# A gated attention layer on one core: x copied into the output early, and the last stage adding to it with accumulating DMAs

## The chip, the core and the metric

The kernel runs on one core of a Trainium2 chip. The core has TensorE (PE in the profile: matmuls; PEld: the loading of their weights), VectorE (DVE), ScalarE (ACT), GpSimd (POOL) and SyncE (SP), and 16 DMA engines that all of them share. SyncE and GpSimd issue the DMAs of this kernel; SyncE's go through the queue that the profile calls q1 (hardware_dynamic), GpSimd's through q0 (software_dynamic). The metric is the device time of one execution in microseconds.

## The reference

For x of 16 sequences of 1024 tokens with 256 features, the output is x plus an attention branch times a gate:

```
xn = layernorm(x)
s  = attention(xn)                        # 16 heads of 16, rope, causal softmax, then @ W_o
h  = leaky(xn @ w_fc[e]) ** 2             # e: the one of 8 experts that the router picks for the token
g  = silu(h @ w_proj[e])
out = x + s * g
```

## The kernel before

The work is cut into 32 tiles (NT) of 512 tokens. A tile in SBUF is 128 partitions by 4 rows of 256 numbers (SUB = 4), 512 KB. Three functions run one after the other.

`project_phase` normalises x, makes q, k, v and the router's choice, and puts each token's row number in the order by experts into `slot` (later called `token_row`).

`attention_phase` goes through 64 groups n, one for each sequence and 4 heads. TensorE makes the scores twice (L1052 for the row maxima, L1118 for the exponentials) and the context (L1094); VectorE takes maxima, ScalarE exponentials. Beside this SyncE works off its own list for each group: `load_max` (L809, 12 KB, which the second scores need), the operands of the group three ahead, `store_ctx` (L813), another `load_max`, another `store_ctx`, and in some groups after that `load_xn` (L816, 512 KB), whose rows GpSimd scatters to their experts (L888).

`expert_output_phase` has two stages. In the first, 72 blocks of 256 tokens go through their experts' weights, and the gates go to `g_dram`, in the order by experts. Meanwhile SyncE loads the context of the first 14 tiles (CR = 14) and x of the first 6 (XR = 6). In the last stage, for each tile t:

- GpSimd issues four indirect DMAs (L1258) that gather the gates of the tile's tokens, 128 rows of 1 KB each, into `gate`, a ring of 4 tiles (GR). Ahead of tile t it waits for `y_used` of tile t-2 (LEAD = 2), the first half of its product.
- TensorE turns the context (L1376) and multiplies it by W_o (L1388) into two halves of 512 columns; ScalarE copies the turned context (L1299).
- VectorE multiplies each half by the gate (L1329, `prod`), waits for x, and adds x in place in `r_sb` (L1334), a ring of 6 tiles.
- SyncE loads the context of tile t+14, stores the tile (L1233) and loads x of tile t+4 (L1210), each as soon as what it needs is there, in this order:

```
            sp.wait_ge(out_ready, 2 * (t + 1))
            sp.dma_start(out[t].rearrange("(s p) d -> p s d", p=P),
                         r_sb[:, t % XR].rearrange("p (s d) -> p s d", s=SUB)).then_inc(out_stored[t % XR], 16)
```

Each engine works off its list in the order in which it is written; semaphores order the engines among each other.

Of the kernel before, what the change touches and what calls it, by code (L numbers as in the profile page):

```python
# [24 lines left out]
ALU = mybir.AluOpType  # L25
ACT = mybir.ActivationFunctionType

P = 128
# [8 lines left out]
SUB = TOK // P  # L37
# [571 lines left out]


def attention_phase(nc, ctx, parts_dram, v_dram, ctx_dram, xn_dram, xs_dram, token_row, w_fc, w_proj, expert_in, first_in,
                    consts):

# [11 lines left out]
    def sem(name):  # L627
        return ctx.enter_context(nc.semaphore(name))
# [47 lines left out]
    scattered = [sem(f"scattered{u}") for u in range(2)]  # L676
    zeros_set = sem("zeros_set")
    xs_cleared = sem("xs_cleared")


    STEPS = []
# [118 lines left out]
    @block.sync  # L800
    def _(sp):
        def load(b, r):
            for i in range(LOADS):
                load_operand(sp, i, parts_dram, v_dram, b, r, q_st[r], k_st[r], v_st[r], operands_loaded[r])

        def load_max(n, r, c):

            sp.wait_ge(max_moved, 2 * n + c + 1)
            sp.dma_start(q_st[r][KS:KM, c, :], max_T[:, c, :]).then_inc(max_loaded[c], 16)  # L809

        def store_ctx(n, b, r, c):
            sp.wait_ge(normalised, 2 * n + c + 1)
            sp.dma_start(ctx_dram[b * TPB + c, :, :, r * GW:(r + 1) * GW], ctx_out[:, c]).then_inc(ctx_stored[c], 16)  # L813

        def load_xn(t):
            sp.dma_start(xn_sb[:, t % 2].rearrange("p s d -> p (s d)"), xn_dram[t]).then_inc(xn_loaded[t % 2], 16)  # L816

        def clear_xs(i):
            sp.dma_start(xs_dram[i * 4 * P:(i + 1) * 4 * P].rearrange("(p a) d -> p (a d)", p=P),
                         zeros[:]).then_inc(xs_cleared, 16)  # L820

        for r in range(1, RING - 1):
            load(0, r)
        load_max(0, 0, 0)
        sp.wait_ge(zeros_set, 1)
        for t in range(2):
            load_xn(t)

        def group(n, b, r, first, last):
            load_max(n, r, 1)  # L830
            r3, b3 = (r + 3) % RING, b + (r + 3) // RING
            if not (isinstance(b3, int) and b3 >= B):
                if not first:
                    sp.wait_ge(pv_done, NS * n)
                load(b3, r3)
            if not first:
                store_ctx(n - 1, b - (1 if r == 0 else 0), (r - 1) % RING, 1)
            if n < CLEAR_GROUPS:
                for i in range(CLEARED // 2):
                    clear_xs(CLEARED * n + i)  # L840
            if not last:
                load_max(n + 1, (r + 1) % RING, 0)
            store_ctx(n, b, r, 0)
            if n < CLEAR_GROUPS:
                for i in range(CLEARED // 2, CLEARED):
                    clear_xs(CLEARED * n + i)
            for s in subs_scattered(n):
                t = s // SUB + 2
                if s % SUB == SUB - 1 and t < NT:
                    sp.wait_ge(scattered[t % 2], 16 * SUB * (t // 2))  # L850
                    load_xn(t)
            if n == EXPERT_WEIGHTS_AT:
                for d in range(DC):
                    sp.dma_start(w_all[:, :, d * HID:(d + 1) * HID],
                                 w_fc[d * P:(d + 1) * P].rearrange("p (e h) -> p e h", e=E)).then_inc(weights_loaded, 16)
                sp.dma_start(w_all[:, :, DC * HID:], w_proj).then_inc(weights_loaded, 16)
            if last:
                for u in range(2):
                    sp.wait_ge(scattered[u], 16 * NT * SUB // 2)
                for m in range(XS):  # L860
                    sp.dma_start(xs_sb[:, m].rearrange("p s d -> p (s d)"), block_rows(xs_dram, m))\
                        .then_inc(xs_loaded[m], 16)

        for n in range(N - RING):
            group(n, n // RING, n % RING, n == 0, False)
        for r in range(RING):
            group((B - 1) * RING + r, B - 1, r, False, r == RING - 1)
        store_ctx(N - 1, B - 1, RING - 1, 1)
        for c in range(HALVES):
            sp.wait_ge(ctx_stored[c], 16 * N)  # L870

# [268 lines left out]
def expert_output_phase(nc, ctx, xs_dram, expert_in, ident, block_expert, g_dram, x, w_o, ctx_dram, token_row,  # L1140
# [10 lines left out]

    RING = 4
    CR, XR = 14, 6
    AHEAD = XR - 2
    LEAD = 2
    BS = BLK // P
    W = SUB * D
# [10 lines left out]
    GR = 4  # L1168
    gate = sb("gate", [P, GR, SUB, D])
    cT = sb("cT", [P, 2, DC, TOK])  # L1170
    prod = sb("prod", [P, 2, W])
    banks = [bank(f"ps_t{i}") for i in range(8)]
    ps_x, ps_h, ps_g = banks[0:2], banks[2:4], banks[4:6]
    ps_cT = [banks[6:8], banks[0:2]]
# [11 lines left out]
    g_stored = [sem(f"g_stored{r}") for r in range(RING)]  # L1186
    wo_loaded = sem("wo_loaded")
    c_loaded = [sem(f"c_loaded{r}") for r in range(CR)]
    x_loaded = [sem(f"x_loaded_o{r}") for r in range(XR)]
    cT_ready = sem("cT_ready")  # L1190
    cT_copied = sem("cT_copied")
    gate_loaded = [sem(f"gate_loaded{r}") for r in range(GR)]
    y_ready = sem("y_ready")
    y_used = sem("y_used")
    out_ready = sem("out_ready")
    out_stored = [sem(f"out_stored{r}") for r in range(XR)]

    block = ctx.enter_context(nc.Block())
# [1 line left out]
    @block.sync  # L1200
    def _(sp):
        def load_xs(n):
            sp.dma_start(xs_sb[:, n % XS].rearrange("p s d -> p (s d)"), block_rows(xs_dram, n))\
                .then_inc(xs_loaded[n % XS], 16)

        def load_ctx(t):
            sp.dma_start(c_sb[:, t % CR], ctx_dram[t]).then_inc(c_loaded[t % CR], 16)

        def load_x(t):
            sp.dma_start(r_sb[:, t % XR].rearrange("p (s d) -> p s d", s=SUB),  # L1210
                         x[t].rearrange("(s p) d -> p s d", p=P)).then_inc(x_loaded[t % XR], 16)

        for n in range(NBLK):
            if n + XS < NBLK:
                sp.wait_ge(xs_turned, n + 1)
                load_xs(n + XS)
            sp.wait_ge(gated, n + 1)
            sp.dma_start(block_rows(g_dram, n), g_sb[:, n % RING].rearrange("p s d -> p (s d)"))\
                .then_inc(g_stored[n % RING], 16)
            if n % 4 == 3 and n // 4 < CR:  # L1220
                load_ctx(n // 4)
            if n == 8:
                sp.dma_start(w_o_sb[:], w_o.rearrange("(c p) n -> p c n", p=P)).then_inc(wo_loaded, 16)
            if n >= NBLK // 2 and n % 4 == 1 and (n - NBLK // 2) // 4 < XR:
                load_x((n - NBLK // 2) // 4)

        for t in range(NT):
            n = t + CR
            if n < NT:
                sp.wait_ge(cT_ready, DC * (t + 1))  # L1230
                load_ctx(n)
            sp.wait_ge(out_ready, 2 * (t + 1))
            sp.dma_start(out[t].rearrange("(s p) d -> p s d", p=P),  # L1233
                         r_sb[:, t % XR].rearrange("p (s d) -> p s d", s=SUB)).then_inc(out_stored[t % XR], 16)
            n = t + AHEAD
            if XR <= n < NT:
                sp.wait_ge(out_stored[n % XR], 16 * (n // XR))
                load_x(n)
        for r in range(XR):
            sp.wait_ge(out_stored[r], 16 * len(range(r, NT, XR)))  # L1240

    @block.gpsimd
    def _(pool):
# [6 lines left out]
                .then_inc(weights_picked, 1)  # L1250
        for r in range(RING):
            pool.wait_ge(g_stored[r], 16 * NBLK // RING)
        for t in range(NT):
            r = t % GR
            if t >= LEAD:
                pool.wait_ge(y_used, 2 * (t - LEAD) + 1)
            for s in range(SUB):
                pool.indirect_dma_start(  # L1258
                    out=gate[:, r, s, :], out_offset=None, in_=g_dram[:, :],
                    in_offset=bass.IndirectOffsetOnAxis(ap=token_row[:, t * SUB + s:t * SUB + s + 1], axis=0))\  # L1260
                    .then_inc(gate_loaded[r], 16)

    @block.scalar
    def _(act):
# [37 lines left out]
    def _(dve):  # L1302
# [19 lines left out]
        for t in range(NT):  # L1322
# [3 lines left out]
            for i in range(2):  # L1326
                cols = slice(512 * i, 512 * (i + 1))
                dve.wait_ge(y_ready, 2 * t + i + 1)
                nc.vector.tensor_tensor(prod[:, u, cols], ps_y[u][i][:], g[:, cols], ALU.mult).then_inc(y_used, 1)  # L1329
            dve.wait_ge(x_loaded[r], 16 * (t // XR + 1))  # L1330
            for i in range(2):
                cols = slice(512 * i, 512 * (i + 1))
                dve.wait_ge(y_used, 2 * t + i + 1)
                nc.vector.tensor_tensor(r_sb[:, r, cols], prod[:, u, cols], r_sb[:, r, cols],  # L1334
                                        ALU.add).then_inc(out_ready, 1)

    @block.tensor
    def _(pe):
# [74 lines left out]
def gated_attention(nc, x, w_all, w_o, w_fc, w_proj, rope, expert_ids, out):  # L1413
# [9 lines left out]
    with ExitStack() as whole:  # L1423
# [6 lines left out]
        expert_in = expert_operands(nc, whole)  # L1430
        with ExitStack() as ctx:
            attention_phase(nc, ctx, parts_dram, v_dram, ctx_dram, xn_dram, xs_dram, token_row, w_fc, w_proj, expert_in,
                            first_in, consts)
        with ExitStack() as ctx:  # L1434
            expert_output_phase(nc, ctx, xs_dram, expert_in, consts[0], block_expert, g_dram, x_t, w_o, ctx_dram,
                                token_row, out_t)
# [41 lines left out]
```

## Time and profile before

| what | value |
|---|---|
| median of 3 runs | 2410.21 us (2407.6 to 2410.84) |
| the profiled execution's own time | 2409.12 us |
| its span, first to last instruction | 2407.4 us |
| mean granted TensorE clock | 0.98 |
| PE, DVE, ACT, POOL busy | 2276.9, 2010.7, 1787.7, 1050.7 us |
| moved by DMA | 406.28 MB |

The span is the profiler's, and 1.7 us of the execution's time lie outside it. Busy times are over all stages: what bounds one stage has to be read from that stage.

### The profile page before, as it was taken

What the parts mean: (1) busy time and instruction counts of PE and PEld (TensorE: products, weight loads), DVE (VectorE), ACT (ScalarE), POOL (GpSimd) and SP (SyncE); (2) the same over time, 40 slices, a digit from 0 to 9 for tenths busy, and PEclk for the clock granted to TensorE, in tenths of its full rate; (3) what the DMA queues carried; (4) which work ended last, traced back from release to release, by engine and by line L of the source; (5) the groups of instructions that cost most, each with busy time, mean ns of one, the idle gap of its engine ahead of it and who ended that gap; (6) DMA issues with size and microseconds to landing.
All of it is one profiled execution on the core that took longest, in us unless ns stands there. A gap on an engine that the chain in (4) does not pass through costs nothing. (4 is left out here: it accounts for less than half of the span.)

```text
span 2407.4 us, 96050 instructions
## 1 busy us (share of the span) xinstructions
PE 2276.9 (95%) x38509; PEld 1342.8 (56%) x38509; DVE 2010.7 (84%) x5739; ACT 1787.7 (74%) x4319; POOL 1050.7 (44%) x1252
## 2 busy tenths in 40 slices
PE   7999994999999999999999999999999999899787
PEld 6777771544545445445454454444454544788676
DVE  7999998999999999999998999999999995454444
ACT  6777771888888888888888888888888888555111
POOL 6999995222223333333333333333332333223666
PEclk9999995999999999999999999999999999999998
DMA  6899885454533433434344334334333331796998
GB/s 215 287 300 301 299 271 164 155 181 164 168 106 99 133 101 103 129 96 128 107 126 130 107 107 127 96 110 124 105 112 111 105 100 30 261 322 246 326 333 262
DMA packets 302572, 406.28 MB, mean 169 GB/s; under 512 B 99248, under 2 KB 233648, under 8 KB 302000
## 3 DMA queue, kind: packets, MB, share of 16 engines
q1 hardware_dynamic: 289840, 366.58, 48.4%
q0 software_dynamic: 12288, 33.57, 4.1%
q8 instruction: 304, 4.98, 0.8%
q14 instruction: 140, 1.15, 0.1%
HBM read 225.46 MB, written 173.02 MB: 166 GB/s over the span
## 5 line engine op out<-in xcount | busy, mean ns | idle before, releaser
L976 DVE CUSTOM_DVE_ANT_0 dump<-ps_rows,mask 128x128 bf16<-128x128 f32 (+7 forms) x2048 | 1471.1, 753 | 132.8 <-issue 108.3
L946 ACT ACTIVATE probs<-ps_cols 128x512 f32<-128x512 f32 (+3 forms) x3072 | 1314.8, 499 | 242.8 <-PE ps_cols L1118 226.5
L1118 PE MATMUL ps_cols<-q_st,k_st 99*32 99x512 bf16 (+3 forms) x12288 | 864.2, 327 | 5.1 <-DMA q_st<-max_T 2.8
L1052 PE MATMUL ps_rows<-k_st,q_st 96*32 96x128 bf16 (+3 forms) x12288 | 817.9, 330 | 18.8 <-DVE row_max L976 7.6
L912 POOL TENSOR_SCALAR_AFFINE_SELECT probs<-probs 128x512 f32<-128x512 f32 x512 | 325.0, 635 | 1039.3 <-ACT probs L946 1034.8
L1094 PE MATMUL ps_ctx<-probs,v_st 128*32 128x512 f32 (+3 forms) x6144 | 633.2, 487 | 1.2 <-POOL probs L912 1.0
L1118 PEld LDWEIGHTS ps_cols<-q_st,k_st 99*32 99x32 bf16 x12288 | 322.1, 95 | 343.7 <-ACT probs L946 173.7
L1052 PEld LDWEIGHTS ps_rows<-k_st,q_st 96*32 96x32 bf16 x12288 | 287.8, 96 | 383.3 <-DVE row_max L976 237.8
L1094 PEld LDWEIGHTS ps_ctx<-probs,v_st 128*32 128x32 f32 x6144 | 168.5, 110 | 92.0 <-POOL probs L912 15.6
L976 DVE DVE_READ_ACCUMULATOR2_ANT row_max<- 128x1 f32 x2048 | 171.8, 84 | 0.0
L1388 PE MATMUL ps_t<-w_o_sb,cT 128*128 128x256 f32 x512 | 128.0, 408 | 31.2 <-DVE prod L1329 29.2
L1258 POOL DMA_INDIRECT gate<-g_dram,slot x128 | 128.5, 1004 | 63.4 <-issue 35.1
L321 POOL TENSOR_TENSOR rest<-roped,parts 128x1024 f32<-128x1024 f32 x64 | 138.2, 2160 | 25.7 <-ACT parts L372 21.1
L888 POOL DMA_INDIRECT xs_dram<-xn_sb,slot x128 | 125.8, 983 | 33.7 <-issue 33.4
L327 POOL TENSOR_TENSOR parts<-rest,parts 128x1024 bf16<-128x1024 f32 x64 | 139.7, 2183 | 0.0
L1299 ACT ACTIVATE cT<-ps_t 128x512 f32<-128x512 f32 x64 | 34.6, 596 | 137.3 <-PE ps_t L1376 137.3
L1329 DVE TENSOR_TENSOR prod<-ps_t,gate 128x512 f32<-128x512 f32 x64 | 41.3, 686 | 112.7 <-DMA gate<-g_dram,slot 112.6
L1388 PEld LDWEIGHTS ps_t<-w_o_sb,cT 128*128 128x128 f32 x512 | 102.6, 206 | 49.7 <-issue 27.6
L378 ACT ACTIVATE parts<-rest 128x1024 bf16<-128x1024 f32 x64 | 67.7, 1058 | 75.7 <-POOL rest L321 75.6
L560 PE MATMUL ps_qk<-xT_hi,w_all_hi 128*128 128x512 f32 x256 | 106.5, 416 | 0.0
L560 PE MATMUL ps_vr<-w_all_hi,xT_hi 128*128 128x264 f32 x256 | 78.3, 306 | 24.0 <-DVE xT_lo L434 23.4
L560 PE MATMUL ps_qk<-xT_hi,w_all_lo 128*128 128x512 f32 x256 | 100.9, 394 | 0.0
(115 smaller groups left out, 2556.5 us busy)
## 6 DMA issues: line engine op xcount, KB each, us to landing
parts_dram<-parts SPq DMA_DIRECT2D x64, 768.0 KB, 4.1
q_st<-parts_dram SPq DMA_DIRECT2D x384, 128.0 KB
k_st<-parts_dram SPq DMA_DIRECT2D x384, 128.0 KB
xs_dram<-zeros SPq DMA_DIRECT2D x36, 512.0 KB, 4.2
xs_sb<-xs_dram SPq DMA_DIRECT2D x72, 256.0 KB, 4.4
g_dram<-g_sb SPq DMA_DIRECT2D x72, 256.0 KB, 3.3
v_dram<-v_sb SPq DMA_DIRECT2D x32, 544.0 KB, 4.9
v_st<-v_dram SPq DMA_DIRECT2D x64, 272.0 KB
```

Of the source, the lines that this page charges most:

```text
L321: nc.gpsimd.tensor_tensor(rest[:, m % 2], roped[:, m % 2].rearrange("p k t -> p (k t)"), parts[:, t % 2, a, 0], ALU.subtract).then_inc(res ...
L327: nc.gpsimd.tensor_tensor(parts[:, t % 2, a, 2], rest[:, m % 2], parts[:, t % 2, a, 1], ALU.subtract).then_inc(part3_done, 1)
L560: mm = nc.tensor.matmul(out, lhs(i, c), rhs(j, c), start=((c, i, j) == PASSES[0]), stop=((c, i, j) == PASSES[-1]))
L888: pool.indirect_dma_start(out=xs_dram[:, :], out_offset=bass.IndirectOffsetOnAxis(ap=token_row[:, s:s + 1], axis=0), in_=xn_sb[:, u, s % S ...
L912: nc.gpsimd.affine_select(out=tri, in_=tri, compare_op=ALU.is_ge, fill=0.0, base=0, pattern=[[0, GH], [1, P]], channel_multiplier=-1).then ...
L946: nc.scalar.activation(probs[:, k % PB, h, 0:w], ps_cols[(GH * k + h) % CB][:, 0:w], ACT.Exp).then_inc(exp_done, 1)
L976: nc.vector.tensor_tensor_reduce(out=dump[:, done % 2, 0:n], in0=ps_rows[:, 512 * bank:512 * bank + n], in1=mask[:, S - n:S], scale=1.0, s ...
L1052: mm = nc.tensor.matmul(ps_rows[a:a + VW, 512 * (bank + c):512 * (bank + c) + w], q_st[r][0:KS, i // IB, q0 + a:q0 + a + VW], k_st[r][0:KS ...
L1094: mm = nc.tensor.matmul(ps_ctx[VW * h:VW * (h + 1), o:o + w], v_st[r][:, j * V_ROW + VP * h:j * V_ROW + VP * h + VW], probs[:, k % PB, h, ...
L1118: mm = nc.tensor.matmul(ps_cols[(GH * k + h) % CB][a:a + VW, 0:w], k_st[r][:, j // IB, k0 + a:k0 + a + VW], q_st[r][:, c, h * 512 + q0 - 5 ...
L1258: pool.indirect_dma_start(out=gate[:, r, s, :], out_offset=None, in_=g_dram[:, :], in_offset=bass.IndirectOffsetOnAxis(ap=token_row[:, t * ...
L1388: mm = nc.tensor.matmul(ps_y[u][i][:, (s % 2) * D:(s % 2 + 1) * D], cT[:, u, c, s * P:(s + 1) * P], w_o_sb[:, c, :], start=(c == 0), stop= ...
```

## The change

x is copied to the output from DRAM to DRAM during attention: SyncE issues a copy of 512 KB at the end of every second group. The last stage then no longer loads x and no longer adds it: VectorE writes the product straight into `r_sb`, and GpSimd issues a DMA for each tile that adds `r_sb` to the output in DRAM (`accum_op`). The ring `prod` and the waits for x go; VectorE waits for a ring place of `r_sb` to have been stored.

```
@@ attention_phase, SyncE
+            if n % TPB == 0:
+                flat = [a[n // TPB].rearrange("(p s) d -> p (s d)", p=P) for a in (out, x)]
+                sp.dma_start(*flat).then_inc(out_filled, 16)
...
+        sp.wait_ge(out_filled, 16 * NT)
@@ expert_output_phase, SyncE
-            if n >= NBLK // 2 and n % 4 == 1 and (n - NBLK // 2) // 4 < XR:
-                load_x((n - NBLK // 2) // 4)
...
-            sp.wait_ge(out_ready, 2 * (t + 1))
-            sp.dma_start(out[t].rearrange("(s p) d -> p s d", p=P),
-                         r_sb[:, t % XR].rearrange("p (s d) -> p s d", s=SUB)).then_inc(out_stored[t % XR], 16)
-            n = t + AHEAD
-            if XR <= n < NT:
-                sp.wait_ge(out_stored[n % XR], 16 * (n // XR))
-                load_x(n)
@@ expert_output_phase, GpSimd
+        def add_out(t):
+            pool.wait_ge(y_used, 2 * (t + 1))
+            pool.dma_start(out[t].rearrange("(s p) d -> p s d", p=P),
+                           r_sb[:, t % XR].rearrange("p (s d) -> p s d", s=SUB), accum_op=ALU.add)\
+                .then_inc(out_stored[t % XR], 16)
+
         for t in range(NT):
             r = t % GR
             if t >= LEAD:
-                pool.wait_ge(y_used, 2 * (t - LEAD) + 1)
+                add_out(t - LEAD)
             for s in range(SUB):
                 pool.indirect_dma_start(
...
+        for t in range(NT - LEAD, NT):
+            add_out(t)
@@ expert_output_phase, VectorE
-                nc.vector.tensor_tensor(prod[:, u, cols], ps_y[u][i][:], g[:, cols], ALU.mult).then_inc(y_used, 1)
-            dve.wait_ge(x_loaded[r], 16 * (t // XR + 1))
-            for i in range(2):
-                cols = slice(512 * i, 512 * (i + 1))
-                dve.wait_ge(y_used, 2 * t + i + 1)
-                nc.vector.tensor_tensor(r_sb[:, r, cols], prod[:, u, cols], r_sb[:, r, cols],
-                                        ALU.add).then_inc(out_ready, 1)
+                if t >= XR:
+                    dve.wait_ge(out_stored[r], 16 * (t // XR))
+                nc.vector.tensor_tensor(r_sb[:, r, cols], ps_y[u][i][:], g[:, cols], ALU.mult).then_inc(y_used, 1)
```

On GpSimd's queue, where the last stage begins, the kernel before has this (the second row of gathers belongs to tiles 0 and 1, the next two to tile 2):

```order
L1249 COPY w_sb<-w_all 128x512
L1258 DMA gate<-g_dram,slot 128x256 [waits g_stored2,g_stored3,g_stored1,g_stored0]
L1258 DMA gate<-g_dram,slot 128x256 x7
L1258 DMA gate<-g_dram,slot 128x256 [waits y_used]
L1258 DMA gate<-g_dram,slot 128x256 x3
```

The changed kernel has in the same place, with line numbers of its own (L1252 is the gather, L1243 the accumulating DMA):

```order
L1237 COPY w_sb<-w_all 128x512
L1252 DMA gate<-g_dram,slot 128x256 [waits g_stored2,g_stored3,g_stored1,g_stored0]
L1252 DMA gate<-g_dram,slot 128x256 x7
L1243 DMA out_dram<-r_sb 128x4x256 [waits y_used]
L1252 DMA gate<-g_dram,slot 128x256 x4
```

The wait for the product now stands on the accumulating DMA, and the four gathers stand behind it; the queue ends with the accumulations of the last two tiles.

On SyncE's queue, in attention, from the second store of a group's context in a group that also loads xn, the changed kernel has this (L814 is the context's store, L817 the load of xn, L810 the load of maxima; the kernel before has the same rows without L855):

```order
L814 DMA ctx_dram<-ctx_out 512x1x64 [waits normalised]
L817 DMA xn_sb<-xn_dram 128x1024 [waits scattered1]
L855 DMA out_dram<-in_x_dram 16x8192
L810 DMA q_st<-max_T 3x16x128 [waits max_moved]
L106 DMA q_st<-parts_dram 16x2x2048 [waits pv_done]
```

The copy stands between the group's last transfers and the next group's load of maxima, 32 times in all.

## Rows read from the trace of the kernel before

**Rows 1.** Stretches: length, busy us (instructions) per engine, PEclk, DMA share, GB/s.

```profile
400.00:1990.00 1590.00, 1575.79 (x33926) 783.60 (x33926) 1461.10 (x4604) 1338.64 (x3333) 510.75 (x742) 0.99 0.40 120
...
2135.00:2213.00 78.00, 76.88 (x423) 65.92 (x421) 39.03 (x71) 46.19 (x108) 20.62 (x34) 1.00 0.86 302
...
2240.00:2270.00 30.00, 24.80 (x133) 21.59 (x133) 12.45 (x20) 5.46 (x11) 20.73 (x21) 1.00 1.00 344
2270.00:2300.00 30.00, 23.02 (x117) 19.73 (x116) 12.45 (x20) 5.42 (x10) 19.87 (x21) 0.94 1.03 365
```

**Rows 2.** The chain that ended last: start us, us, what it followed.

```profile
2301.72 7.52 DMA gate<-g_dram,slot
2310.23 0.95 POOL gate L1258
...
2314.15 7.22 DMA gate<-g_dram,slot
...
2350.74 1.22 POOL gate L1258
2353.51 0.95 POOL gate L1258
```

**Rows 3.** Groups of instructions: busy us, mean ns, idle us before them and releasers.

```profile
L1258 POOL DMA_INDIRECT gate<-g_dram,slot x128 | 128.5, 1004 | 63.4 <-issue 35.1 <-DVE prod L1329 17.5 <-DMA g_dram<-g_sb 10.9
...
L1329 DVE TENSOR_TENSOR prod<-ps_t,gate 128x512 f32<-128x512 f32 x64 | 41.3, 686 | 112.7 <-DMA gate<-g_dram,slot 112.6
L1334 DVE TENSOR_TENSOR r_sb<-prod,r_sb 128x512 f32<-128x512 f32 x64 | 41.1, 684 | 0.0
```

**Rows 4.** Timeline of the last stage, its beginning and end: start us, us, instructions.

```profile
2217.70 1.04 POOL L1258 DMA_INDIRECT gate<-g_dram,slot  x1 [10.86 <-DMA g_dram<-g_sb]
...
2382.96 0.38 SPq L1233 DMA_DIRECT2D out_dram<-r_sb  x1
...
2387.18 17.16 SPq L1233 DMA_DIRECT2D out_dram<-r_sb  x4
...
2397.79 0.95 POOL L1258 DMA_INDIRECT gate<-g_dram,slot  x1 [0.30 <-issue]
2401.45 1.29 DVE L1329 TENSOR_TENSOR prod<-ps_t,gate 128x512 f32<-128x512 f32 x2 [4.19 <-DMA gate<-g_dram,slot]
2402.66 1.28 DVE L1334 TENSOR_TENSOR r_sb<-prod,r_sb 128x512 f32<-128x512 f32 x2
```

**Rows 5.** DMA from 2240 to 2390 us: packets, MB, share; last row median us to landing.

```profile
q1 hardware_dynamic: 30029, 35.64, 69.8%
q0 software_dynamic: 5043, 13.76, 28.2%
...
r_sb<-in_x_dram SPq DMA_DIRECT2D x25, 512.0 KB, 7.1
```

**Rows 6.** Timeline of SyncE's queue in attention.

```profile
1002.87 0.63 SPq L816 DMA_DIRECT2D xn_sb<-xn_dram  x1
1007.76 0.75 SPq L809 DMA_DIRECT2D q_st<-max_T  x1
...
1033.05 0.74 SPq L809 DMA_DIRECT2D q_st<-max_T  x1
...
1053.53 0.63 SPq L816 DMA_DIRECT2D xn_sb<-xn_dram  x1
1058.41 0.75 SPq L809 DMA_DIRECT2D q_st<-max_T  x1
```

**Rows 7.** DMA issues of the whole kernel: count, KB each, median us to landing.

```profile
x_sb<-in_x_dram SPq DMA_DIRECT2D x32, 512.0 KB, 6.7
...
out_dram<-r_sb SPq DMA_DIRECT2D x32, 512.0 KB, 4.6
```

**Rows 8.** Timeline of TensorE in the last stage, one tile.

```profile
2349.39 1.04 PE L1376 MATMUL ps_t<-ident_f,c_sb 128*128 128x128 f32 x8
2350.26 3.62 PE L1388 MATMUL ps_t<-w_o_sb,cT 128*128 128x256 f32 x16
```

More of the change, by code:

```diff
@@ L611, in attention_phase @@
 def attention_phase(nc, ctx, parts_dram, v_dram, ctx_dram, xn_dram, xs_dram, token_row, w_fc, w_proj, expert_in, first_in,
-                    consts):
+                    consts, x, out):
     def sb(name, shape, dt=F32):
@@ L678, in attention_phase @@
     xs_cleared = sem("xs_cleared")
+    out_filled = sem("out_filled")
     STEPS = []
@@ L1153, in expert_output_phase @@
     CR, XR = 14, 6
-    AHEAD = XR - 2
     LEAD = 2
@@ L1170, in expert_output_phase @@
     cT = sb("cT", [P, 2, DC, TOK])
-    prod = sb("prod", [P, 2, W])
     banks = [bank(f"ps_t{i}") for i in range(8)]
@@ L1188, in expert_output_phase @@
     c_loaded = [sem(f"c_loaded{r}") for r in range(CR)]
-    x_loaded = [sem(f"x_loaded_o{r}") for r in range(XR)]
     cT_ready = sem("cT_ready")
@@ L1194, in expert_output_phase @@
     y_used = sem("y_used")
-    out_ready = sem("out_ready")
     out_stored = [sem(f"out_stored{r}") for r in range(XR)]
@@ L1207, in load_ctx @@
             sp.dma_start(c_sb[:, t % CR], ctx_dram[t]).then_inc(c_loaded[t % CR], 16)
-        def load_x(t):
-            sp.dma_start(r_sb[:, t % XR].rearrange("p (s d) -> p s d", s=SUB),
-                         x[t].rearrange("(s p) d -> p s d", p=P)).then_inc(x_loaded[t % XR], 16)
         for n in range(NBLK):
@@ L1432, in gated_attention @@
             attention_phase(nc, ctx, parts_dram, v_dram, ctx_dram, xn_dram, xs_dram, token_row, w_fc, w_proj, expert_in,
-                            first_in, consts)
+                            first_in, consts, x_t, out_t)
         with ExitStack() as ctx:
```

## The prediction

> **What bounds the kernel now.** I read the table of stretches first. Attention, from 400 to 1990 us, keeps TensorE busy for 1575.79 of 1590 us with the DMA engines at 0.40; the expert stretch before 2213 us is TensorE's too (76.88 of 78 us, DMA 0.86). In the last stage it turns over: from 2240 to 2300 us the DMA engines stand at 1.00 and 1.03, and TensorE is busy for 24.80 and 23.02 of 30 us [rows 1]. The chain that ended last says how that is felt. It alternates between GpSimd, which issues the gathers of the gates, and a DMA wait of about 7 us until a tile's last gather has landed; each such pair covers two tiles in about 12 us, because the gathers of tile t wait for the product of tile t-2. From about 2346 us, with the ctx loads over, it runs for long stretches from one of GpSimd's gathers to another [rows 2]. VectorE waits 112.6 us for gathers, and its sums (L1334) wait for nothing [rows 3].
>
> So two resources are nearly full. **GpSimd:** the 128 gathers take 128.5 us of busy time, and 35.1 us more go between them with nothing waited for, 0.30 us each time. That is 163.6 us of its own, 1.28 us per gather and 5.11 per tile; it waits for the product 17.5 us [rows 3, 4]. The sum, 181.1 us, is the time from the first gather's start at 2217.7 to the last one's end at 2398.7. **DMA:** from 2240 to 2390 us q1 (SyncE's transfers) took 69.8% of 150 us, 104.7 us, for 35.64 MB, so 1.54 us of all engines for one 512 KB tile; q0 (gathers) took 28.2%, 42.3 us, for 13.76 MB, so 1.61 us [rows 5]. A tile costs 1.54 (x) + 1.54 (store) + 1.61 (gathers) = 4.69 us, and 6.23 where a ctx load is added (18 of the 32 tiles), 5.56 us on average, against a pace of 181.1/32 = 5.66. The end, 2398.7 to 2407.4, is 8.7 us: landing, two products, two sums, store [rows 4].
>
> **The change, part by part.**
>
> *Copies of x in attention:* 32 of 512 KB, on SyncE behind a ctx store, 16 rows of 32 KB each. In that very place the kernel already loads 512 KB of xn in some groups. The next load of maxima, the small transfer that TensorE needs, comes 4.9 us later (1002.87 to 1007.76, 1053.53 to 1058.41), and a group with such a load lasts as long as one without: these maxima are loaded at 1007.76, 1033.05 and 1058.41, 25.29 and 25.36 us apart, the xn load lying in the second interval alone [rows 6]. The copy is from DRAM to DRAM, which no row shows; its price is between 1.54 us of the engines and the 6.7 us that a load of x takes to land [rows 7]. I take the double pass, 3.1 us, under the 4.9: nothing. With 6.7 the cover is gone by 1.8 us, 32 times 1.8 = 58 us.
>
> *x loads gone:* six lay beside the experts, where TensorE is full, so nothing is gained; 26 lay in the last stage. *Sums gone:* 64 of 0.684 us, 41.1 us [rows 3], all but the last two while VectorE would wait for gathers; the last tile's are in the tail.
>
> *Stores become accumulating DMAs on GpSimd.* This carries the sum. Each of the 32 now stands on GpSimd's queue ahead of the next tile's four gathers, and waits for both halves of the product of tile t-2, where the gathers waited for one. Call A what one costs GpSimd, gap included. No row shows one. The low end is a store's issue on SyncE, 0.38 us [rows 4]; the high end is four gathers, 5.11 us, since a tile has 512 rows of 1 KB like four gathers. I take 1.9 us, half as much again as one gather: nearest to one instruction, because the rows' addresses follow a regular pattern and no row numbers have to be read for them, but with something added for four times the rows.
>
> The Trainium skill (DMA: Bandwidth & Descriptors, Anatomy of one DMA — SWDGE (gpsimd) path) says that generating descriptors is a small, variable part, and that many can be emitted before the added cost shows. By that rule the 512 rows would cost what the 128 of one gather cost, A = 1.28, and the sum below would be 2431; all gathers here have 128 rows, so no row shows it.
>
> *DMA work:* an accumulating DMA reads both sides and writes one; I count it as the load and the store it replaces, 3.08 us (low end a store alone, 1.54; high end the 7.1 us in which a load of x landed under load [rows 5]). Then a tile costs the engines 5.56 us as before, 6.23 with a ctx load.
>
> *The new pace:* GpSimd needs 5.11 + 1.9 = 7.0 us a tile, above the engines' 6.23 and above TensorE's, for which the rows have 3.62 + 1.04 = 4.66 us a tile [rows 8]. GpSimd becomes the bound. Its wait for the product mostly vanishes: between the last gather of t and the accumulation of t lie one accumulation and four gathers, 7.0 us, while landing and product need 2.7 + 1.3 = 4.0 (as at the end) to 7.0 + 1.3 = 8.3 us (under load) [rows 2, 4]. I take nothing for it.
>
> *Sum:* from the first gather to the last one's end lie 30 accumulations: 163.6 + 30 x 1.9 = 220.6 us, against 181.1: +39.5. The tail: landing 2.7, products 1.3, A 1.9, landing of the accumulation 4.6 (a store's median over the kernel [rows 7]; the last one now lands in about 3): 10.5 against 8.7, +1.8. Together +41.3 on the profiled execution's 2409.12, which is 1.1 us under the median of the runs: **2450.4 us, +1.7%**.
>
> **Rivals.**
>
> 1. *Row by row:* descriptors priced like a gather's. For: a tile's rows equal four gathers'. Against: the gather has row numbers to read. At A = 5.11, 163.6 + 153.3 = 316.9, +135.8, tail +5: 2550. At A = 2.6: 2472.
> 2. *The DMA engines bind.* An accumulation that reads its target before it writes could hold them longer than a load and a store. It decides from 7.0 - 1.61 - 0.87 = 4.5 us each (0.87 is the ctx load spread over the tiles). At 7.1 us a tile costs 9.6 us, 307 us for 32: +126, and 2537. For: these engines are the full resource now. Against: 1.54 us per 512 KB counts passes, and three passes would be 4.6.
> 3. *Not slower:* the accumulation costs GpSimd what a store costs SyncE, 0.38 us [rows 4]. Break-even is A = (181.1 - 163.6)/30 = 0.58 us. With 0.4, 163.6 + 12 = 175.6, and if the accumulation costs the DMA engines less than load plus store, the gathers land sooner and hardly wait: 2404 to 2410. Against: nothing GpSimd issues here takes under 0.95 us [rows 4].
> 4. *A cheaper accumulation, 0.58 to 1.28:* the same sum gives 2410 to 2431. For: the SyncE end of the bounds. Against: it would undercut every gather.
> 5. *The copies delay the maxima in attention:* up to 58 us, with the rest about 2508. Against: the xn loads in the same place leave no trace.
>
> **How the numbers follow.** A between 1.28 and 2.6, 2431 to 2472: 0.50. Rival 1: 0.16. Rival 2: 0.13. Rival 3: 0.08. Rival 4: 0.08. Rival 5: 0.05. The forecast is 2450. The range leaves out rival 3, half of rival 4 and the far ends of rivals 1 and 2, together about 2 in 10: 2420 to 2515. A measurement of this kernel tells about 0.2%, 4.8 us, from no change. Rival 3 and the low end of rival 4 share 0.03 faster and 0.06 within it; all the rest is slower by more, 0.91.
>
> **What would show it.** In the profile after: GpSimd without long waits from 2217 us on, the accumulation's duration (A less 0.30 us) beside the gathers' unchanged 0.95, a pace near 7 us a tile; DMA engines under 0.95; VectorE's 64 products waiting for gathers still, without sums; the attention stretch of the same length and the first gather within a few us of 2217.7. The prediction is wrong if the accumulation takes GpSimd under 0.6 or over 3 us, if GpSimd waits on VectorE for long with the DMA engines full (rival 2), or if the first gather comes late (rival 5).

## The result and the profile after

The changed kernel takes **2446.71 us** (median of 4 runs, 2445.31 to 2447.70) against 2408.90 us of the kernel before in the same comparison: a ratio of 1.0164, 95% interval 1.0138 to 1.0190. That is slower by 1.6%. The profiled execution took 2447.57 us; its span is 2445.8 us, 38.4 more than before.

I read the same views as ahead of the prediction. First the table of stretches (length, busy us and instructions of PE, PEld, DVE, ACT and POOL, granted clock, DMA share, GB/s), in the last stage of the changed kernel:

```profile
2240.00:2270.00 30.00, 19.52 (x95) 16.32 (x93) 6.04 (x10) 4.34 (x8) 24.52 (x23) 0.94 1.03 234
2270.00:2300.00 30.00, 22.94 (x125) 19.79 (x124) 5.56 (x9) 5.42 (x10) 24.52 (x24) 1.00 1.03 239
2300.00:2330.00 30.00, 21.45 (x102) 17.95 (x100) 5.15 (x8) 5.43 (x10) 24.53 (x23) 0.89 1.05 235
2330.00:2360.00 30.00, 25.15 (x120) 21.56 (x120) 6.44 (x10) 4.49 (x9) 24.53 (x24) 0.89 0.86 165
2360.00:2390.00 30.00, 19.46 (x104) 16.46 (x103) 6.44 (x10) 5.28 (x10) 24.52 (x23) 1.00 0.82 150
```

GpSimd's column (POOL, the last pair of busy time and count) stands at 24.52 or 24.53 us in every stretch, where it was 20.73 and 19.87 in [rows 1]. The DMA share falls from 1.05 to 0.86 when the ctx loads end at about 2330 us, and GpSimd does not move faster for it. GB/s fell from 344 and 365 to 234 and 239 at the same share, so a byte now costs the DMA engines more.

The groups of instructions (busy us, mean ns, idle us before them and what ended it) say that GpSimd waits for almost nothing ("issue" is time in which the profile shows nothing that the engine waited for, here the gaps of 0.30 us between its instructions):

```profile
L1252 POOL DMA_INDIRECT gate<-g_dram,slot x128 | 127.2, 994 | 49.4 <-issue 38.5 <-DMA g_dram<-g_sb 10.8
L1243 POOL DMA_DIRECT2D out_dram<-r_sb x32 | 46.7, 1458 | 2.0 <-DVE r_sb L1327 1.9
L1327 DVE TENSOR_TENSOR r_sb<-ps_t,gate 128x512 f32<-128x512 f32 x64 | 41.2, 685 | 177.7 <-DMA gate<-g_dram,slot 177.7
```

The 17.5 us for which the gathers waited for the product [rows 3] are gone; one wait of 1.9 us is left, at the very end. In their place stand 46.7 us of accumulating DMAs, 1.46 us each. VectorE's products wait 177.7 us for gathers instead of 112.6.

The timeline of GpSimd's queue and of VectorE (start us, us, instructions, idle before in brackets), at the beginning, for one tile, and at the end:

```profile
2223.26 1.03 POOL L1252 DMA_INDIRECT gate<-g_dram,slot  x1 [10.85 <-DMA g_dram<-g_sb]
...
2233.10 1.48 POOL L1243 DMA_DIRECT2D out_dram<-r_sb  x1
...
2299.73 1.46 POOL L1243 DMA_DIRECT2D out_dram<-r_sb  x1
2301.50 1.06 POOL L1252 DMA_INDIRECT gate<-g_dram,slot  x1 [0.31 <-issue]
2302.86 1.02 POOL L1252 DMA_INDIRECT gate<-g_dram,slot  x1 [0.30 <-issue]
2304.18 0.96 POOL L1252 DMA_INDIRECT gate<-g_dram,slot  x1 [0.30 <-issue]
2305.45 0.96 POOL L1252 DMA_INDIRECT gate<-g_dram,slot  x1 [0.30 <-issue]
2306.41 1.46 POOL L1243 DMA_DIRECT2D out_dram<-r_sb  x1
...
2432.01 0.96 POOL L1252 DMA_INDIRECT gate<-g_dram,slot  x1 [0.31 <-issue]
2432.97 1.46 POOL L1243 DMA_DIRECT2D out_dram<-r_sb  x1
2434.76 1.29 DVE L1327 TENSOR_TENSOR r_sb<-ps_t,gate 128x512 f32<-128x512 f32 x2 [5.32 <-DMA gate<-g_dram,slot]
2436.35 1.31 POOL L1243 DMA_DIRECT2D out_dram<-r_sb  x1 [1.92 <-DVE r_sb L1327]
```

From one accumulation to the next are 6.68 us here: four gathers of 1.06, 1.02, 0.96 and 0.96, the accumulation of 1.46, and four gaps of 0.30, with none between a gather and the accumulation. That is the pace of the whole stage: from 2233.10 to 2432.97 us lie 30 such steps, 6.66 us each. The chain that ended last has the same pieces one behind the other, with no DMA among them, where the chain before went through DMA waits of 7 us [rows 2] (start us, us, what it followed):

```profile
2305.45 0.96 POOL gate L1252
2306.41 1.46 POOL out_dram L1243
2308.18 1.06 POOL gate L1252
```

So the 38.4 us are made up of three parts. The first gather starts at 2223.26 instead of 2217.70: **+5.6**. From it to the last one's end are 209.7 us instead of 181.1: **+28.6**. From there to the span's end are 12.8 us instead of 8.7: **+4.1**.

The DMA queues from 2240 to 2420 us (packets, MB, share of the engines' time; last row count, KB each, median us to landing):

```profile
q0 software_dynamic: 19510, 28.49, 82.6%
q1 hardware_dynamic: 1949, 7.07, 11.4%
...
out_dram<-r_sb POOLq DMA_DIRECT2D x28, 512.0 KB, 6.4
```

q0 took 82.6% of 180 us, 148.7 us, for some 27 tiles. With 1.61 us for a tile's gathers, as before, 105 us are left for the accumulations: an estimate of 3.85 us of all engines for each. Behind the last gathers, from 2436 us on, accumulations were alone in flight (the same view of that stretch):

```profile
q0 software_dynamic: 979, 0.97, 67.4%
```

That is 6.6 us of the 9.8 up to the span's end for 0.97 MB, an estimate of 3.6 us for 512 KB with no gather beside them.

### The profile page after: what moved, and what is told of

It is laid out like the page before. It is cut to its first block and busy times, and to the rows that moved or that the text cites. A ratio compares the mean times of both kernels' runs of the same rounds, so it can differ in the third digit from the quotient of the medians.

```text
span 2445.8 us, 95979 instructions
## 1 busy us (share of the span) xinstructions
PE 2280.8 (93%) x38508; PEld 1342.4 (55%) x38509; DVE 1971.5 (81%) x5675; ACT 1787.5 (73%) x4319; POOL 1096.1 (45%) x1284
## 5 line engine op out<-in xcount | busy, mean ns | idle before, releaser
L1057 PE MATMUL ps_rows<-k_st,q_st 96*32 96x256 bf16 (+3 forms) x12288 | 818.7, 330 | 18.2 <-DVE row_max L981 7.6
L1327 DVE TENSOR_TENSOR r_sb<-ps_t,gate 128x512 f32<-128x512 f32 x64 | 41.2, 685 | 177.7 <-DMA gate<-g_dram,slot 177.7
L1252 POOL DMA_INDIRECT gate<-g_dram,slot x128 | 127.2, 994 | 49.4 <-issue 38.5
```

The costliest lines, as they stand in the source:

```text
L1057: mm = nc.tensor.matmul(ps_rows[a:a + VW, 512 * (bank + c):512 * (bank + c) + w], q_st[r][0:KS, i // IB, q0 + a:q0 + a + VW], k_st[r][0:KS ...
L1252: pool.indirect_dma_start(out=gate[:, r, s, :], out_offset=None, in_=g_dram[:, :], in_offset=bass.IndirectOffsetOnAxis(ap=token_row[:, t * ...
```

## The experiments

My theory after this result: GpSimd's time to issue sets the pace of the last stage. The rival: the DMA engines set it, since they stood at 1.03 for half of it, and GpSimd looks busy because its DMAs are taken on slowly. The first four kernels ran on one chip (the kernel before: 2409.34 us there), the last three on another (2407.73).

**The copies alone.** The kernel before, and in attention the 32 copies of x; its output is overwritten by the last stage's stores.

```
+            if n % TPB == 0:
+                flat = [a[n // TPB].rearrange("(p s) d -> p (s d)", p=P) for a in (out, x)]
+                sp.dma_start(*flat).then_inc(out_filled, 16)
```

> The kernel before with the 32 copies of x into the output during attention, and nothing else changed (the last stage still loads x and stores over the copies). My theory (GpSimd's issuing sets the pace of the last stage; the copies cost once, about 3 us, in the one group where the experts' weights are loaded right behind a copy): 2412, a ratio of 1.001 to before, and the load of maxima late in that group alone. If the copies carry all of the 5.6 us by which the last stage of the changed kernel begins later: ratio 1.0023. If they are hidden altogether: 1.000.

Measured: 2411.42 us, ratio 1.0010 (0.9999 to 1.0021). The copies cost between nothing and 0.2%; rival 5's 58 us are excluded. Its trace has the late start of the last stage all the same:

```profile
2224.31 1.04 POOL L1263 DMA_INDIRECT gate<-g_dram,slot  x1 [10.86 <-DMA g_dram<-g_sb]
L1263 POOL DMA_INDIRECT gate<-g_dram,slot x128 | 128.6, 1005 | 58.9 <-issue 34.1 <-DVE prod L1334 13.9 <-DMA g_dram<-g_sb 10.9
```

The first gather starts 6.6 us later than in the kernel before, but from there to the last one's end are 176.6 us instead of 181.1, with 13.9 us of waiting for the product instead of 17.5. So in this trace most of a late start was made up in the last stage. Where the late start comes from is looked for with the fourth kernel.

**A plain store from GpSimd.** The changed kernel without `accum_op`: the stores leave x out of the output.

```
-                           r_sb[:, t % XR].rearrange("p (s d) -> p s d", s=SUB), accum_op=ALU.add)\
+                           r_sb[:, t % XR].rearrange("p (s d) -> p s d", s=SUB))\
```

> The changed kernel with a plain DMA from GpSimd in the place of the accumulating one (x is then left out of the result). If the issue on GpSimd sets the pace, the 1.46 us stay and so does the pace of 6.66 us a tile: 2441 to 2445, the gain only in the landing of the last one. If the accumulation's hold on the DMA engines (about 3.85 us a tile) sets it, a plain store holds them about 1.5 us, the pace falls to GpSimd's or the engines' old one, near 5.7 us, and the time to about 2415.

Measured: 2420.62 us, ratio 1.0052 (1.0032 to 1.0072). This was not foreseen: the plain store took GpSimd 0.80 us, not as long as the accumulation. The kernel's groups, one stretch and one tile's timeline:

```profile
L1243 POOL DMA_DIRECT2D out_dram<-r_sb x32 | 25.8, 806 | 2.6 <-DVE r_sb L1327 2.5
```

```profile
2360.00:2390.00 30.00, 23.58 (x125) 20.12 (x124) 6.44 (x10) 5.43 (x10) 23.61 (x26) 1.00 0.57 176
```

```profile
2302.57 0.80 POOL L1243 DMA_DIRECT2D out_dram<-r_sb  x1
...
2308.42 0.81 POOL L1243 DMA_DIRECT2D out_dram<-r_sb  x1
```

A tile takes 5.85 us here, and GpSimd still waits for nothing but 2.5 us, once, with the DMA engines at 0.57. By itself the kernel tells the theories apart only through that trace, because both the issue and the work of the DMA engines became cheaper at once.

**Fewer, longer rows.** The changed kernel with 128 rows of 4 KB in each accumulation instead of 512 of 1 KB; it adds the products to other tokens' rows.

```
-            pool.dma_start(out[t].rearrange("(s p) d -> p s d", p=P),
-                           r_sb[:, t % XR].rearrange("p (s d) -> p s d", s=SUB), accum_op=ALU.add)\
+            pool.dma_start(out[t].rearrange("(p s) d -> p (s d)", p=P), r_sb[:, t % XR], accum_op=ALU.add)\
```

> The changed kernel with accumulating DMAs of 128 rows of 4 KB instead of 512 rows of 1 KB (the products are added to other tokens of the same tile). If the issue's price is per row, the 1.46 us fall to about 0.4, the pace to 5.6 and the time to about 2412. If most of it is a fixed part, as the rule says that many descriptors can be emitted before their cost shows, it stays at 1.3 to 1.5 and the time at 2441 to 2446. I expect a mixture, 1.0 us and 2432.

Measured: 2433.89 us, ratio 1.0103 (1.0082 to 1.0124).

```profile
L1243 POOL DMA_DIRECT2D out_dram<-r_sb x32 | 32.6, 1018 | 2.9 <-DVE r_sb L1326 2.8
```

The issue fell from 1.46 to 1.02 us. Over 30 accumulations that is 13.2 us, and the time fell by 12.8 (medians of two comparisons). So 512 rows of 1 KB cost GpSimd 0.44 us more than 128 rows of 4 KB, and what the issue lost the kernel gained. The work of the DMA engines became cheaper here too, though less than in the plain store (a share of 0.97 to 0.99 until 2330 us, where the changed kernel has 1.03 to 1.05), so this kernel speaks for the issue by the size of the gain alone.

**The copies in the other groups.** The changed kernel with the copies one group later, so that none stands ahead of the loads of the experts' weights.

```
-            if n % TPB == 0:
+            if n % TPB == 1:
```

> The changed kernel with the copies in the odd groups instead of the even ones, so that none stands right ahead of the experts' weights. If that one meeting costs 3 us: 3 us under the changed kernel, 2443.5, a ratio of 1.015 to before, and no wait of TensorE for the maxima there. If the copies cost in every group or not at all: no difference to the changed kernel.

Measured: 2447.70 us, ratio 1.0164 (1.0147 to 1.0182), so no gain in the time. In its trace the stall is gone all the same. This is SyncE's queue in the changed kernel, where the experts' 2 MB of weights (L858, L860) are loaded:

```profile
1256.05 0.63 SPq L855 DMA_DIRECT2D out_dram<-in_x_dram  x1
1256.72 1.33 SPq L858 DMA_DIRECT2D w_all<-in_w_fc_dram  x2
1258.10 2.22 SPq L860 DMA_DIRECT2D w_all<-in_w_proj_dram  x1
1260.92 1.32 SPq L810 DMA_DIRECT2D q_st<-max_T  x1
...
1283.21 0.80 SPq L810 DMA_DIRECT2D q_st<-max_T  x1
```

and what TensorE waited for there (us in total, times, longest):

```profile
PE ps_cols L1123 <- DMA q_st<-max_T: 1.8, 1, 1.8
...
PEld ps_cols L1123 <- DMA q_st<-max_T: 2.2, 1, 2.2
```

From one load of maxima to the next this group takes 22.29 us; with the copies elsewhere it takes 18.96:

```profile
1262.81 0.78 SPq L810 DMA_DIRECT2D q_st<-max_T  x1
...
1281.77 0.79 SPq L810 DMA_DIRECT2D q_st<-max_T  x1
```

Here the first gather starts at 2221.48, 1.8 us sooner than in the changed kernel, and the span is 2444.3 against 2445.8 us. That can't be put down to the move. The kernels below with the longer lead and with two halves have the copies where the changed kernel has them, ran on the other chip, and start the last stage at 2221.22 and 2221.01. Their group is short too; this is the one with the longer lead:

```profile
1261.49 0.95 SPq L810 DMA_DIRECT2D q_st<-max_T  x1
...
1281.38 0.80 SPq L810 DMA_DIRECT2D q_st<-max_T  x1
```

The group takes 19.89 us there and 20.12 with two halves, against 22.05, 21.84 and 22.80 in the first three kernels. So copies ahead of the weights cost this group about 3 us in the changed kernel and on the first chip, a little over 1 us on the other (where it takes 18.70 in the kernel before with the longer lead, without copies), and the time does not show either.

**A longer lead, before and after.** Here GpSimd waits for the product of tile t-3 instead of t-2, in both kernels. If GpSimd never waits in the changed kernel, that changes nothing there.

```
-    LEAD = 2
+    LEAD = 3
```

> The kernel before with LEAD = 3: the gathers of tile t wait for the product of tile t-3 instead of t-2, nothing else. If the last stage of the kernel before was held by the wait of about 7 us in its chain (gather, landing, product, next gather), this loosens it: down to what GpSimd (163.6 us) or the DMA engines (178 us) need, 2 to 10 us less, 2400 to 2407, ratio 0.996 to 0.999. If the DMA engines were the bound throughout, no change.

> The changed kernel with LEAD = 3. If GpSimd's own instructions set its pace, it waits for nothing already, and the time stays within 2 us of the changed kernel, 2445 to 2449 (one accumulation more stands behind the last gathers). If its last stage were held by the loop from gather over product to the next gather, loosening it would bring it down by 10 us or more.

Measured: the kernel before with the longer lead takes **2398.01 us, ratio 0.9958 (0.9943 to 0.9973)**, faster than both kernels of this case. The changed kernel with it takes 2447.45 us, ratio 1.0167 (1.0147 to 1.0186), no change. The first kernel's groups, one of its stretches, and the same stretch of the kernel before:

```profile
L1258 POOL DMA_INDIRECT gate<-g_dram,slot x128 | 129.8, 1014 | 49.5 <-issue 34.1 <-DMA g_dram<-g_sb 10.9 <-DVE prod L1329 4.6
```

```profile
2300.00:2330.00 30.00, 25.26 (x136) 21.50 (x135) 13.84 (x23) 6.51 (x12) 23.20 (x23) 1.00 1.06 394
```

```profile
2300.00:2330.00 30.00, 24.71 (x127) 21.50 (x126) 12.48 (x20) 5.42 (x10) 19.89 (x21) 0.94 1.00 338
```

GpSimd's wait for the product falls from 17.5 to 4.6 us, and the same DMA engines move 394 GB/s in this stretch where they moved 338. From the first gather's start to the last one's end are 168.5 us instead of 181.1, 5.3 a tile, and 163.9 of them are GpSimd's own.

In the changed kernel with the longer lead the accumulations wait once, for 0.6 us:

```profile
L1243 POOL DMA_DIRECT2D out_dram<-r_sb x32 | 46.6, 1476 | 0.7 <-DVE r_sb L1327 0.6
```

**Each accumulation in two halves.** The changed kernel, with two accumulating DMAs of 256 rows for each tile: the bytes and rows stay, GpSimd issues one more instruction.

```
+            for half in (slice(0, 2), slice(2, 4)):
+                pool.dma_start(to[:, half], of[:, half], accum_op=ALU.add).then_inc(out_stored[t % XR], 16)
```

> The changed kernel with each accumulating DMA issued as two of half a tile, 256 rows each, behind the same wait: the DMA engines get the same rows, GpSimd two instructions. From 1.46 us for 512 rows and 1.02 for 128, an instruction has a fixed part of 0.87 and 1.15 ns a row: two halves cost 2.33 us, the pace rises from 6.66 to 7.5 us a tile and the time by 26 to 28, to 2473. If the DMA engines set the pace, it stays at 6.66 and the time at 2447. If the price were per row alone, two halves would cost GpSimd the same as one whole, and the time would stay too.

Measured: 2483.03 us, ratio 1.0312 (1.0292 to 1.0333). GpSimd's timeline and one stretch:

```profile
2301.61 2.63 POOL L1246 DMA_DIRECT2D out_dram<-r_sb  x2
2304.55 1.07 POOL L1253 DMA_INDIRECT gate<-g_dram,slot  x1 [0.30 <-issue]
...
2309.46 2.63 POOL L1246 DMA_DIRECT2D out_dram<-r_sb  x2
```

```profile
2360.00:2390.00 30.00, 22.25 (x96) 18.23 (x94) 4.09 (x7) 4.34 (x8) 25.44 (x24) 0.84 0.77 134
```

The pace went to 7.85 us a tile while the DMA share fell, in this stretch from 0.82 in the changed kernel to 0.77. Two halves cost 2.63 us instead of 1.46: 30 x 1.17 = 35 us, and the time stands 35.6 us above that of the changed kernel with the longer lead, on the same chip. The rival, by which the same bytes and rows take the same time, is out. The size I had expected, 26 us, was too small: I had drawn a line through the two prices that I had, 1.02 us for 128 rows and 1.46 for 512, which gives 1.17 for 256; half of a pair is 1.31 us. The two prices differ in the length of the rows as well, so the line was a rough estimate.

## Why the prediction was right

The forecast was 2450 us, +41.3 on the profiled execution; measured were +38.4. The mechanism was that of the forecast, GpSimd as the bound. Three terms of its sum were off: one by 10.9 us too much, two by 7.9 too little together. That the total came within 2.9 us is in part luck.

- **A, the accumulation's cost on GpSimd**, was taken as 1.9 us. The runs give 209.7 - 163.6 = 46.1 us for 30 of them, 1.54 each: 1.46 of issue, and the gaps and slower gathers around it. That is 10.9 us less than the sum had. The high bound, the price of four gathers, was far off. The reason that I gave, that more rows cost a little more, holds: 1.02 us for 128 rows and 1.46 for 512. But a plain store of the same 512 rows takes 0.80, so accumulating them adds 0.66. The profile's packets on GpSimd's queue qualify that (whole kernel: before, changed, plain store):

```profile
q0 software_dynamic: 12288, 33.57, 4.1%
q0 software_dynamic: 29184, 50.35, 9.0%
q0 software_dynamic: 16896, 50.35, 6.3%
```

  Above the 12288 of the indirect DMAs, one accumulation of 512 rows makes 528 packets; the plain store of the same rows makes 144. The kernel with rows of 4 KB has 16896 packets too, so its accumulations also make 144 each. At 144 packets each, accumulating takes 1.02 us against 0.80. Whether the packets are what costs GpSimd the rest is not shown.
- **The Trainium skill's rule** that I weighed against it would have had 1.28 for A, and 2431 us. 1.54 lies between that and my 1.9, nearer to that rule. The Trainium skill (DMA: Bandwidth & Descriptors, Anatomy of one DMA — SWDGE (gpsimd) path) says that many descriptors can be emitted before the added cost shows; the traces agree in part: four times the rows cost 1.4 times as much, not four times, but the 0.44 us are there in every tile.
- **GpSimd's wait for the product vanishes**: right. 17.5 us before, one wait of 1.9 after, at the very end, and a longer lead changes nothing. "I take nothing for it" held although the DMA engines were fuller than forecast.
- **X, the work of an accumulation for the DMA engines**, was taken as 3.08 us, a load and a store; the estimate from the trace is 3.85. So "DMA engines under 0.95" was wrong until 2330 us (1.03 to 1.05). Rival 2 was to decide from 4.5 us, and by 3.85 it came close: 3.85 + 1.61 + 0.87 = 6.33 us a tile against GpSimd's 6.66. The 0.87 spreads the ctx loads over all tiles; while they last a tile costs 3.85 + 1.61 + 1.54 = 7.00, so by this estimate the engines were at least as full as GpSimd until 2330 us. That they did not set the pace is shown twice: it is 6.66 in that half and stays there when the share falls to 0.82, and in the kernel with two halves it gets slower while the engines have more room. The DMA work that the forecast gave the kernel before was too high as well: the 5.56 us a tile count all 32 loads of x, and with the 26 that lay in the last stage the same prices give 76 x 1.54 + 32 x 1.61 = 168.6 us, 5.27 a tile.
- **Copies: nothing** was nearly right in the time: with the copies alone it is 2.08 us above that of the kernel before, with an interval that just holds no change. But the first gather came 5.6 us late, the sign that the forecast had named for rival 5, at a tenth of that rival's size. The rows that I had read (a group with an xn load takes as long as one without) did not cover the one group in which 2 MB of weights follow on the same queue. There the maxima come late, and the group is 3.1 us longer than before (19.21 us from 1260.96 to 1280.17 there). Another 0.8 us lie elsewhere in attention, and 1.7 between attention and the first gather, 1.3 of them behind the experts' first matmul. There TensorE's granted clock came back later: 0.50 from 2058 to 2062 and 0.75 from 2062 to 2066 in the changed kernel, whose experts start at 2058.02, against 0.62 from 2054 to 2058 and 1.00 from 2058 to 2062 in the kernel before, where they start at 2053.80 (0.50 is the level of 1.2 GHz, 0.62 and 0.75 are means over both levels). TensorE had idled for about as long in both (6.71 and 6.64 us). Why it rose later is not settled, and it need not be the copies: this piece, from the experts' first matmul to the first gather, takes from 163.9 to 165.2 us over the nine traces, and 163.9 and 164.5 in the two without copies. The 5.6 us are those of one pair of traces: the first gather starts at 2217.70 and 2219.39 without copies and between 2221.0 and 2224.3 with them.
- **The tail** was taken as 10.5 us and came to 12.8. The products stand 1.8 us behind the last gather, not 2.7, and take 1.6 with the gap behind them. The last accumulation's issue and landing took 6.5, which is just the 1.9 + 4.6 of the forecast, though an accumulation's median is 6.4 and a store's 4.6. What the sum did not have is the piece behind that landing: 3.0 us up to the span's end, where the kernel before has 0.45. The profile shows a DRAIN there, the instruction with which GpSimd's list ends (count, then ns min/median/max, first and last start; the first row is the landing of the last accumulation, from its start at 2436.35; the last row is of the kernel before):

```profile
DMA to landing us min/median/max: 6.5/6.5/6.5
L1426 POOLq DRAIN  x1: 9281/9281/9281, 2436.3 to 2436.3; - x1
...
L1434 POOLq DRAIN  x1: 10316/10316/10316, 2392.1 to 2392.1; - x1
```

  In the changed kernel it ends at 2445.6 us, 2.7 behind the landing at 2442.9; in the kernel before it ended at 2402.5, ahead of the last store's landing at 2406.9. What it waits for in these 2.7 us is not shown.
- **x loads and sums gone: nothing gained**: right. VectorE lost the 41.1 us of sums and waits 65 us longer for gathers.
- Rival 4's upper end (A = 1.28) came within 0.3 us of A; rival 3 (below 0.58) did not come near. A plain store on the same queue would have been rival 4, at 2420.62 us.

So the sum reads: 41.3 - 10.9 for A, + 5.6 for the late start, + 2.3 for the tail, 38.3 us.

## What to carry to other kernels

An operation that is moved to a queue whose engine already issues for 5.1 of 5.7 us in each round costs its issue time in every round, however much work it takes from other engines: find that queue's own time, without its waits, and add to it. Price a kind of DMA that the trace does not have from both sides, and price its issue and its time on the DMA engines apart, since here the issue alone set the pace while the engines' share went from 1.05 to 0.82. Before replacing the work around a wait, try to wait for an older item: here the longer lead gave 0.42% in the kernel before, by a change of one number.

## What the runs showed of the hardware that I had not expected

- Accumulating is dearer to issue than storing: 1.46 us against 0.80 on GpSimd's queue for the same 512 rows of 1 KB. Accumulating 128 rows of 4 KB took 1.02. Two accumulations of 256 rows, one right behind the other, took 2.63 together; their records overlap, so this is not the price of a single one. By these numbers most of the price does not go with the rows.
- It is dearer to carry out than a load and a store together: an estimate of 3.85 us of all engines for 512 KB, and of 3.6 with no gather beside it, where those took 1.54 each [rows 5].
- The first gather behind an accumulation takes 1.06 us and the second 1.00 to 1.02; behind a plain store they take 0.98 and 0.96.
- A DMA share of 1.00 to 1.03 did not mean that the engines could give no more: with a longer lead the stretch from 2300 to 2330 us moved 394 GB/s at 1.06, where it had moved 338 at 1.00. It does not follow that the engines had room left at the end: by the prediction's prices the DMA work of that stage is 168.6 us (with 26 loads of x), and its gathers took 168.5 from the first's start to the last's end. Whether GpSimd, which needs 163.9 of them, or the engines hold the kernel with the longer lead, no run tells.
- The six kernels here that end with a DMA of GpSimd's went on for 3.0 to 3.6 us after it had landed, the three that end with a DMA of SyncE's for 0.4 to 0.6.
